# Position bias and relative attention in one block with shared memory, and semaphores that count from zero

## What is computed

```python
qkv = (x @ w_qkv.T).reshape(B, N, 3, H, hd).transpose(2, 0, 3, 1, 4)   # B 4, N 1024, H 16, hd 16
q, k, v = (qkv[0] * scale, qkv[1], qkv[2])
attn = jnp.einsum('bhid,bhjd->bhij', q, k)
idx = (jnp.clip(arange(N)[None, :] - arange(N)[:, None], -31, 31) + 31)[None, None]
qL = jnp.einsum('bhid,hdm->bhim', q, rpe_k_table)              # m: 63 buckets
attn = attn + jnp.take_along_axis(qL, idx, axis=-1)
kL = jnp.einsum('bhjd,hdm->bhjm', k * scale, rpe_q_table)
attn = attn + jnp.swapaxes(jnp.take_along_axis(kL, idx, axis=-1), 2, 3)
attn = jax.nn.softmax(attn, axis=-1)
out = jnp.einsum('bhij,bhjd->bhid', attn, v)                   # plus the values' position table
return x_out @ w_proj.T + b_proj
```

## Time and profile before

| | |
|---|---|
| median of 3 runs | 2425.92 us (2425.19 to 2429.5) |
| the profiled execution, its own time | 2436.6 us |
| its span, first to last instruction | 2434.7 us |
| PE / DVE / ACT / POOL busy | 2030.2 / 1617.5 / 1234.3 / 493.8 us |
| mean granted TensorE clock | 0.924 of 2.4 GHz |
| preparation | 0 to 35 us |
| feed-forward 0, local attention, feed-forward 1 | 37 to 180, 181 to 801, 805 to 948 us |
| bit 0, projection | 949 to 1021, 1023 to 1140 us |
| bias, its last stores and barrier | 1142 to 1290, to 1308 us |
| relative attention | 1308 to 2367 us |
| bit 1 | 2371 to 2433 us |

### The profile page before, as it was taken

The page is one execution under the profiler, slowest core; times in us unless marked ns, Lnnn a source line. Parts: engine busy times, 40 slices in busy tenths (PEclk is TensorE's granted clock), DMA queues, the critical chain, the costliest instruction groups (busy, mean ns, idle before and its releaser), DMA issues. The chain is left out here.

```text
span 2434.7 us, 74675 instructions
## 1 busy us (share of the span) xinstructions
PE 2030.2 (83%) x32204; PEld 1285.8 (53%) x32280; DVE 1617.5 (66%) x2553; ACT 1234.3 (51%) x1862; POOL 493.8 (20%) x794
## 2 busy tenths in 40 slices
PE   3986887888887796497773999999999999999975
PEld 2654555556455564354673555555555555555544
DVE  6775354453533677774353888888888888888847
ACT  3761221223212575322330677767777777777754
POOL 0002000000000000000001554444543454435410
PEclk7998999998989898698886899999999999999996
DMA  3001000000000000133237555544555455545412
GB/s 106 1 1 43 3 1 19 2 19 3 1 19 2 1 1 5 25 122 114 105 149 244 148 139 135 137 123 118 135 136 136 131 138 134 132 125 135 110 31 74
DMA packets 273793, 195.13 MB, mean 80 GB/s; under 512 B 206744, under 2 KB 260310, under 8 KB 273210
## 3 DMA queue, kind: packets, MB, share of 16 engines
q1 hardware_dynamic: 262586, 139.27, 22.5%
q0 software_dynamic: 10496, 50.75, 5.5%
q10 hardware_dynamic: 384, 0.33, 0.1%
HBM read 91.69 MB, written 93.88 MB: 76 GB/s over the span
## 5 line engine op out<-in xcount | busy, mean ns | idle before, releaser
L2020 DVE TENSOR_REDUCE a1c_nm<-a1c_S 128x1 f32<-128x1024 f32 x512 | 609.6, 1218 | 98.9 <-PE a1c_S L2105 98.3
L1960 ACT ACTIVATE a1c_PT<-a1c_ST 128x1024 f32<-128x1024 f32 x499 | 510.3, 1023 | 57.5 <-PE a1c_ST L2105 54.7
L1975 ACT ACTIVATE a1c_Pb<-a1c_S,a1c_nm 128x192 f32<-128x192 f32 (+1 forms) x512 | 212.9, 416 | 217.7 <-DVE a1c_nm L2020 216.7
L1904 POOL TENSOR_TENSOR a1c_lt<-a1c_lt 128x256 f32<-128x256 f32 (+5 forms) x448 | 254.7, 568 | 35.4
L2010 DVE COPY a1c_PbT<-a1c_T 96x512 f32<-96x512 f32 x256 | 175.7, 686 | 96.1 <-PE a1c_T L2137 93.7
L2105 PE MATMUL a1c_S<-a1c_KR,a1c_Q 54*32 54x512 f16 (+13 forms) x2816 | 180.7, 316 | 19.7 <-DMA a1c_Gx<-a_bias 18.3
L2105 PE MATMUL a1c_ST<-a1c_Q,a1c_KR 57*128 57x256 f16 (+2 forms) x1066 | 175.0, 284 | 22.3 <-ACT a1c_PT L1960 21.5
L2105 PE MATMUL a1c_S<-a1c_KL,a1c_Q 54*32 54x512 f16 (+11 forms) x3136 | 191.8, 323 | 0.6 <-ACT a1c_Pb L1975 0.3
L2105 PE MATMUL a1c_S<-a1c_Gx,ident 64*32 64x96 f32 (+2 forms) x4352 | 184.8, 240 | 0.0
L1896 POOL DMA_DIRECT2D a_band<-a1c_Pb x128 | 71.4, 558 | 495.6 <-ACT a1c_Pb L1975 495.3
L2137 PE MATMUL a1c_T<-ident,a1c_Pb 128*96 128x128 f32 x1024 | 168.1, 288 | 0.8 <-DVE a1c_mhl L2034 0.8
(11 more groups left out here) (344 smaller groups left out, 4138.4 us busy)
## 6 DMA issues: line engine op xcount, KB each, us to landing
a_band<-a1c_Pb POOLq DMA_DIRECT2D x128, 384.0 KB, 3.3
a_bias<-a1b_G SPq DMA_DIRECT2D x32, 768.0 KB, 8.1
a1c_Gx<-a_bias SPq DMA_DIRECT2D x128, 192.0 KB, 4.3
a1c_Dt<-a_band SPq DMA_DIRECT2D x128, 126.0 KB, 3.7
a1c_Q<-a_qk SPq DMA_DIRECT2D x192, 64.0 KB
a1c_Vw<-a_values SPq DMA_DIRECT2D x64, 102.0 KB, 2.8
a1c_KL<-a_qk SPq DMA_DIRECT2D x96, 64.0 KB
a1c_KR<-a_qk SPq DMA_DIRECT2D x90, 64.0 KB
```

What stands on the lines that cost most here:

```text
L1904: add = lambda o, x, y: nc.gpsimd.tensor_tensor(o, x, y, ALU.add)
L1960: nc.scalar.activation(PT[:, q % 8, :, :], place(q), ACT.Exp).then_inc(s["exp"], 1)
L1975: nc.scalar.activation(Pb[:, band_slot(I, c), w0:w1], SP[:, t % 2, I * P - 32 + w0:I * P - 32 + w1], ACT.Exp, bias=nm[:, t // 16 % 2, col: ...
L2020: nc.vector.tensor_reduce(nm[:, t // 16 % 2, col:col + 1], SP[:, t % 2, :], AX.X, ALU.max, negate=True).then_inc(s["max"], 1)
```

## The change

1. **Semaphores.** `ONE` and `arm` are gone; every wait `ONE + k` is a wait for `k`. `sems` no longer clears. SyncE clears a block's semaphores during the next block (`clear_old`), and they are released after it (`turn_over`). In the feed-forward blocks and in the attention block that is the first thing SyncE does, in the others it comes after the block's first loads. One block at the very end clears the last block's 27.
2. **One block for bias and attention.** `rel_bias` becomes a class `Bias` whose parts are called at the start of each engine's queue in `rel_attend`. Its tile `a1b_G` and its PSUM share memory with the tiles of the attention, and new waits stand where the barrier stood: for the queries (`wait_queries`), the sums (`wait_sums`), the copies (`wait_copies`) and the stores of one unit (`wait_out`). Six tiles of `rel_attend` are declared in another order, so that those over `a1b_G` are the ones that wait for a store.
3. **Order of the bias units.** The query steps of units 0 and 2 run alone, ahead of that unit's key steps, in turn in the banks `a1b_q` and `a1b_k`, and their four copies are shared, two on ScalarE and two on VectorE. The query steps of units 1 and 3 stay between the key steps of the unit before, with four copies on ScalarE.
4. **SyncE's order at the start of the attention.** Queries and keys of group 0 wait for the last query step only. The last unit's store comes after both halves of `Gx`. `b_proj` and the loads of group 1 wait for that store to land.

The diff without the waits that only lose their `ONE +`, and cut:

```diff
-def arm(sp, s):
-    for x in s.values():
-        sp.sem_inc(x, ONE)
...
+def clear_old(G, sp):
+    for x in G.old:
+        sp.sem_clear(x)
...
+def turn_over(nc, G):
+    for x in G.old:
+        nc.release_semaphore(x)
+    G.old, G.live = G.live, []
...
+class Bias:
...
+    def alone(self, u):
+        return u % 2 == 0
...
+    def banks(self, u, st):
+        return self.pk if self.alone(u) and st % 2 == 1 else self.pq
...
+    def store(self, sp, u):
+        m, half = divmod(u, 2)
+        if u >= 2:
+            self.wait_out(sp, u - 2)
+        sp.wait_ge(self.s["kev"], self.NK * (u + 1))
+        for h in range(8):
+            sp.dma_start(self.GD[8 * m + h, :, :]...
...
+        for u in range(self.NU):
+            if self.alone(u):
+                for st in range(NQ):
+                    by_query(u, st)
+            for i in range(NQ):
+                for x in range(3):
+                    by_key(u, 3 * i + x)
+                if u + 1 < self.NU and not self.alone(u + 1):
+                    by_query(u + 1, i)
...
         def _(sp):
-            arm(sp, {n: x for n, x in s.items() if n not in ("pw0", "pw1", "k0_in")})
-            sp.dma_start(bp[:, :], A["b_proj"].partition_broadcast(P)).then_inc(s["bp_in"], 16)
+            clear_old(G, sp)
+            bias.sync(sp)
...
+            bias.wait_queries(sp)
             load_queries(0, 0)
             load_keys(0)
             sp.wait_ge(s["zero"], 1)
+            bias.wait_out(sp, 0)
+            bias.wait_out(sp, 1)
             load_bias(0, 0)
             load_queries(0, 1)
             load_bias(0, 1)
+            bias.last_out(sp)
+            bias.wait_out(sp, 2)
             load_values(0)
             load_windows(0, 0)
+            bias.wait_out(sp, 3)
+            sp.dma_start(bp[:, :], A["b_proj"].partition_broadcast(P)).then_inc(s["bp_in"], 16)
             load_keys(1)
             load_queries(1, 0)
             load_windows(0, 1)
...
         def _(pool):
-            nc.gpsimd.memset(Gx[:, :, 8, :], 0.0).then_inc(s["zero"], 1)
+            bias.wait_queries(pool)
...
+            bias.wait_sums(pool)
+            nc.gpsimd.memset(Gx[:, :, 8, :], 0.0).then_inc(s["zero"], 1)
...
+                if q == 0:
+                    bias.wait_out(act, 2)
+                    bias.wait_out(act, 3)
...
+            bias.tensor(pe)
+            bias.wait_sums(pe)
+            bias.wait_copies(pe)
```

More of the change, by code:

```diff
@@ L78, in prep_phase @@
         pa = ctx.enter_context(nc.psum_tensor("pa0", [P, 512], F32))
[L79 removed]
+        s = sems(nc, G, "prep", "w1_in w2_in b1_in b2_in zero ident ones abs1 abs2 neg signs1 signs2 diag tr evac bcast a2h b2h sums stat "
                  + " ".join(f"x_in{i}" for i in range(NC)))
@@ L143, in aggregate @@
             def aggregate(i):
-                dve.wait_ge(s["sums"], ONE + i + 1)
+                dve.wait_ge(s["sums"], i + 1)
                 for t in range(CT):
@@ L205, in ffn_phase @@
         psY = ps("psY", [P, 2, CT, D])
-        s = sems(nc, ctx, f"ffn{r}", "eps sd rstd xn xT xhi xlo xb H h hhi hlo Y scaled out sums stat")
+        s = sems(nc, G, f"ffn{r}", "eps sd rstd xn xT xhi xlo xb H h hhi hlo Y scaled out sums stat")
         block = ctx.enter_context(nc.Block())
@@ L498, in _ @@
             nc.gpsimd.memset(blk[:, :], 1.0).then_inc(s["zero"], 1)
-            pool.wait_ge(s["zero"], ONE + 1)
+            pool.wait_ge(s["zero"], 1)
             c = Count(s["masks"])
@@ L518, in _ @@
             nc.gpsimd.memset(lmaskT[:, :], 0.0).then_inc(s["zero"], 1)
-            pool.wait_ge(s["zero"], ONE + 3)
+            pool.wait_ge(s["zero"], 3)
             for half in range(2):
@@ L574, in _ @@
                 xT_out(0, g4)
-            act.wait_ge(s["sels"], ONE + 5)
-            act.wait_ge(s["zero"], ONE + 2)
+            act.wait_ge(s["sels"], 5)
+            act.wait_ge(s["zero"], 2)
             for j in range(EARLY):
@@ L731, in _ @@
             pool_rows(0)
-            dve.wait_ge(s["zero"], ONE + 3)
+            dve.wait_ge(s["zero"], 3)
             for b in range(B):
@@ L1281, in rel_project @@
         eps = sb("eps", [P, 1])
-        s = sems(nc, ctx, "a1p", "eps sd rstd w_in p_in tab_in rv_in zero clear const tab ends rv wtr wev xn xT xTev Q Qf Qhi Qlo V Vev E Ehi Elo "
+        s = sems(nc, G, "a1p", "eps sd rstd w_in p_in tab_in rv_in zero clear const tab ends rv wtr wev xn xT xTev Q Qf Qhi Qlo V Vev E Ehi Elo "
                  "e_out0 e_out1 q_out v_out0 v_out1 pad_out pads strip c_out")
@@ L1886, in _ @@
             nc.gpsimd.memset(VL[:, :, :, :, :], 1.0).then_inc(s["zero"], 1)
-            pool.wait_ge(s["zero"], ONE + 4)
+            pool.wait_ge(s["zero"], 4)
             def store(g):
@@ L1940, in _ @@
         def _(act):
+            bias.scalar(act)
+            bias.wait_queries(act)
             for g in range(2):
@@ L2002, in _ @@
         def _(dve):
+            bias.vector(dve)
             def band_out(d):
@@ L2356, in macaron_kernel, with _ @@
             prep_phase(nc, G, A)
+            turn_over(nc, G)
             for ph in PHASES[:3][:STOP]:
                 ph(nc, G, A)
+                turn_over(nc, G)
         for ph in PHASES[3:STOP]:
             ph(nc, G, A)
+            turn_over(nc, G)
+        block = ctx.enter_context(nc.Block())
+        @block.sync
+        def _(sp):
+            clear_old(G, sp)
 STOP = 99
```

812 lines of the change are left out of this document (417 added, 395 removed).

## The result

| | before | changed kernel |
|---|---|---|
| median beside each other | 2427.71 us (2425.19 to 2431.48, 4 runs) | 2360.59 us (2353.14 to 2365.43, 4 runs) |
| ratio | 1 | 0.972 (95% interval 0.969 to 0.975) |
| profiled execution, own time / span | 2436.6 / 2434.7 us | 2365.43 / 2363.7 us |
| mean granted TensorE clock | 0.924 | 0.942 |

It is faster by 2.8%, where 3.1% was forecast, and inside the range. The forecast's own ratio is 2351.4 / 2425.92 = 0.9693. Both measurements are above it, the second by 0.0002 only, and both intervals hold the forecast. The stages say more than the total.

What follows compares the result with a forecast made beforehand. No single engine bounds all nine blocks; TensorE holds the long attention loop, and the gain lies in holes elsewhere. 15.5 + 3.7 + 35.0 + 29.3 - 7 - 2 = 74.5 us less gives 2351.4 us; range 2336 to 2370.

Steps and rivals of the forecast that it cites:

- Clears, -15.5: Between blocks: 227 semaphore clears and seven barrier releases leave the path, 15.5 us less.
- counting from zero, -3.7: Before first loads: SyncE's additions of 16 vanish, paying only in preparation and projection, 3.7 us less.
- Bias stage, -35.0: Bias stage: new unit order and shared copies shorten it from 148.5 to 113.5 us, 35.0 less (31 to 38).
- some 5: Sign of being right, bias stage: ScalarE waits for a store once, some 5 us.
- The rival of a whole store wait: Bias stage: a whole store wait stays, 16 us at most given back, 2365 us; chance 0.07.
- From the last sum to the first score, -29.3: Seam from bias to attention: the gap falls from 36.6 to 7.3 us (to 8.5), 29.3 less.
- Wrong: a first-score gap above 12 us: Sign of being wrong: the first attention score comes more than 12 us after the last bias sum.
- What is late next, +7: Attention's pass 10: SyncE sends shift rows late, TensorE stands 6 to 8 us, +7 us (0 to 12).
- The clock, +2: Attention after the stall at pass 10: full clock comes some us later, +2 us (0 to 6).
- The rule on the clock: Start of attention: by activity alone dense passes free the clock and the +2 us vanishes; not counted on.
- Rival 2: Attention's dense passes: clock stays at half, six such passes cost some 20 us, 2371 us; chance 0.09.
- granted clock 0.5: Sign of being wrong: TensorE's granted clock is 0.5 in the attention loop.

Runs made afterwards that it cites:

- Experiment 2: Kernel before with both semaphore parts only (clears moved, counting from zero), separate blocks and old unit order; 2413.37 us, ratio 0.9912.
- Experiment 1: Kernel before with counting from zero only, clears where they were; 2435.12 us beside 2432.31, ratio 0.9995.
- the control: The changed kernel run once more, unedited, in another group of runs; 2359.70 us, ratio 0.9695 to the kernel before.
- experiment 7: Changed kernel with unit 2's store sent behind the loads of group 0's queries and keys; 2365.46 us, ratio 0.9731.
- experiment 10: Changed kernel with the 18 loads of group 0's queries and keys issued by ScalarE instead of SyncE; 2357.55 us, ratio 0.9687.
- experiment 6: Changed kernel without ScalarE's wait for the last bias sums ahead of its first exponentials; 2361.87 us, ratio 0.9721.
- experiment 8: Changed kernel with shift rows sent earlier, exponentials' table ahead of its waits and unit 2's store behind group 0's loads; 2360.05 us, ratio 0.971.
- experiment 11: Changed kernel with group 0's queries and keys loaded by ScalarE, group 1's by GpSimd, exponentials' table ahead of its waits; 2349.71 us, ratio 0.9652.
- experiment 3: Kernel before with the new order of bias units only, in its own block, semaphores as before; 2401.89 us, ratio 0.9873.
- experiment 4: Changed kernel with the old unit order and all copies on ScalarE, merging and semaphores kept; 2400.07 us, ratio 0.9859.

## Why the prediction was right, and where a step was off

- **Clears, -15.5, and counting from zero, -3.7.** Preparation, both feed-forwards, bit 0, the projection, local attention and the attention loop were to give 19.2. Experiment 2 gave 19 us in the total. Experiment 1 showed 1.5 and 2.2 us of the second term in its two stages (1.6 and 2.1 forecast); in its total nothing shows. Right.
- **Bias stage, -35.0.** 148.6 to 112.6 us, -36.0; -34.2 alone. By its parts: first sum 10.4 us in (11.6 forecast); a copy pair on VectorE 1.02 us (1.1 taken); unit 1's sums 19.5; one store wait, which costs VectorE 3.75 us (5 forecast); ScalarE stands 9.28 us for it, not the "some 5" that the signs named. The rival of a whole store wait is out. Right.
- **From the last sum to the first score, -29.3.** Measured -24.5 and, in the control, -25.6: 12.1 and 11.0 us stand where 7.3 was forecast. This is the term that was mis-sized, and the step is "only GpSimd's clearing and the five loads of Gx are behind the last sum". I had taken the loads of group 0 as done by then, at the issue times they have with nothing in flight. The eight issues of unit 2's store take 10.05 us instead of 8.23 and the loads behind them 12.9 instead of 8, together more than unit 3's 19.4 us of sums. So 3.8 us pass before `Gx` is asked for, and the first score comes 5.5 us after the issue of its last part instead of 3.8. Experiments 7 and 10 add that neither order nor queue bought more than about 1 us of it: asked for 3.2 us sooner, `Gx` took at least 1.4 us longer to land. The cause is argued from the share of the DMA engines (0.91 and 0.87 in the two windows ahead of the first score), which the store's 6.3 MB and then the small loads fill; no run moved fewer bytes. Where SyncE's code was the same, the gap still varied from 10.4 to 12.1 us. "Wrong: a first-score gap above 12 us" is thus just met in this profile (12.1) and not in the control.
- **What is late next, +7.** The stall at the shift rows is 8.1 us (control 9.3), for the reason given. The last store landed 19.0 us after its first issue (16.2 forecast), 21.5 us after the first score (20.3), and the rows left 35.3 us after it (31.6 to 33.9). The maxima themselves come 1.2 us later than forecast (27.1 us after the first score, 25.9 before). That is the table load, which I had not seen: an added wait on ScalarE took that load with it, and in experiments 6, 8 and 11, without that wait, the maxima are at 25.9 again. Together +9.4 us to the first by-key product.
- **The clock, +2.** From the first by-key product to the second shift rows it is 28.9 us, +3.0. But the mechanism was wrong. The kernels without a stall (0.2 us at most), experiments 1, 2 and 3, have 28.7 to 28.8 us too. The profile of before was the odd one: its clock was at 1.00 from 1356.8 on, the very time of its first by-key product. In all thirteen other profiles the last rise comes 14 us or more after that product, with or without a stall. So the term is a property of the one profile that I compared with.
- **The rule on the clock.** I had set the Trainium skill, "TensorE: Matmul & The Clock Gate", What's actually happening (activity releases the half clock) aside. In the changed kernel TensorE is busy 13.39 of 14.60 us right behind the stall and is granted 0.50 for all of it, so by that stretch too the rule as worded is not enough; then it rises and stays. Rival 2 had this mechanism with six dense passes; here it was three, and "granted clock 0.5" in the loop, a sign of being wrong, was there for these 14.2 us.
- **What no term had.** Local attention is 8.3 us shorter in the profile, 3.6 of it at its end, where the clears were (4.07 us from its last instruction to the next stage's first, now 0.50). The other 4.7 go with less low clock in code that did not change (75 us against 94).

By stage, profile to profile: clears and zero about -18.6, bias -36.0, gap -24.5, to the first by-key +9.4, from there to the end of the loop +3.4 beside its clears, local attention's clock -4.7: -71 us, against -74.5 forecast. The 3.5 us between them are the gap (+4.8), the stall and the table load (+2.4), the loop (+1.4) and the clears (+0.6), less the bias (1.0) and local attention's 4.7. The merging alone, forecast at 20.3 us with its stall and its clock, gave 11.7 by these rows and some 13 by experiment 4; a term that nobody had forecast makes up for more than half of that. A forecast within 4 us therefore owes something to luck. The range has a slip: the ends of the terms as given add up to -60 and -88 us, not -56; the measured -67 lies inside either.

## What to carry to other kernels

When a barrier between two stages is removed, add up the bytes and the small loads still in flight at the new seam before pricing the first loads behind it. Durations of DMA issues are only good at the load of the DMA engines under which they were read. For a queue that sends everything in one fixed order, list all users behind the moved block, not just the next one: removing the first late transfer here made the next one late, by more. And a term of 2 or 3 us that rests on one profile's clock should be looked for in a second kernel first.

## What was not expected of the hardware

- With a unit's store in flight the issue of a load on SyncE takes 1.3 us (three in 4.01, at 1226.03) instead of 0.4 to 0.5 (three in 1.24 to 1.64 in the kernel before). ScalarE's eight loads of constants slow down likewise, 8.2 us against 3.4 before. The DMA share is 0.87 to 1.04 in these stretches.
- The granted clock fell soon after TensorE went idle, at 1239.1 (idle since about 1235.9), and stayed low for 61.4 us; 64.9 in the control, which was idle no longer (10.3 us against 11.4). In the kernel before, the low stretch was 64.9 us as well.
- The same local attention took 604 us with 50 us at low clock and 617 with 84. What sets these stretches was not tried and stays open.
